# Second attention of a one-core decoder block: maxima subtracted through extra rows of the stacks, stacks copied by halves of the heads, score units further ahead, bias additions at another place

## The reference

```python
Q = query @ Wq.T + bq;  K = key @ Wk.T + bk;  V = value @ Wv.T + bv      # 16 heads of 8
energy = jnp.einsum('bhqd,bhkd->bhqk', Q, K) / jnp.sqrt(jnp.float32(HD))
attn = jax.nn.softmax(energy, axis=-1)
x = jnp.einsum('bhqk,bhkd->bhqd', attn, V)
return x @ Wo.T + bo
x = _layernorm(x + _L0_xattn_ref(x, ctx_1024, ctx_1024, ...), axis=-1)
```

## Time and profile before

| | us |
|---|---|
| median of 3 runs | 356.65 (356.54 to 357.73) |
| the profiled execution's own time | 357.19 |
| its span in the profile | 355.4 |
| PE busy / DVE / ACT / POOL | 326.9 / 250.7 / 190.7 / 215.4 |

### The profile page before, as it was taken

One profiled execution on the slowest core, in us unless ns is written; L12 is line 12 of the kernel. 1 busy time (PEld: TensorE's weight loads), 2 busy tenths in 40 slices (PEclk: granted clock), 3 DMA queues, 4 the chain that ended last, 5 costly groups with the idle time before them and its releaser, 6 DMA issues.

```text
span 355.4 us, 11656 instructions
## 1 busy us (share of the span) xinstructions
PE 326.9 (92%) x3728; PEld 259.1 (73%) x3728; DVE 250.7 (71%) x1220; ACT 190.7 (54%) x458; POOL 215.4 (61%) x402
## 2 busy tenths in 40 slices
PE   6989899998999999975799999998889999999993
PEld 3877788887888888864588887887646765666662
DVE  1688899988989999966367767769754279254454
ACT  3586566766676665575677767754643342222220
POOL 8375899998889977788733343311134445554552
PEclk9999999999999999999999999999999999999998
DMA  7669797775677688545454544641055300624310
GB/s 219 191 188 307 233 268 229 231 223 166 202 201 208 179 235 236 168 130 140 115 133 115 145 116 99 164 106 46 10 175 183 87 32 7 180 88 144 122 32 30
DMA packets 67808, 54.07 MB, mean 152 GB/s; under 512 B 29617, under 2 KB 57649, under 8 KB 67633
## 3 DMA queue, kind: packets, MB, share of 16 engines
q1 hardware_dynamic: 67328, 52.43, 51.9%
q10 hardware_dynamic: 432, 1.05, 0.9%
HBM read 33.40 MB, written 20.05 MB: 150 GB/s over the span
## 4 chain that ended last, share of the span: by engine, by line
PE 45%; POOL 16%; issue 11%; DVE 9%; DMA 9%; ACT 4%; SPq 4%; POOLq 0%; ACTq 0%; DVEq 0%
PE bank L844 6%; PE bank L1109 5%; DMA parts_dram<-parts 4%; PE bank L1113 4%; PE bank L784 4%; PE bank L1122 4%; DMA stk<-parts_dram 2%; PE bank L773 2%; POOL rstd L562 2%; PE bank L799 2%; POOL rest L498 2%; DMA sup_w<-in_sup_w_dram 2%; PE bank L828 2%; PE bank L821 2%; PE bank L787 2%
## 5 line engine op out<-in xcount | busy, mean ns | idle before, releaser
L707 POOL TENSOR_TENSOR stk<-stk 128x512 f32<-128x512 f32 x32 | 40.8, 1274 | 38.3 <-ACT stk L1434 35.4
L1227 ACT ACTIVATE prob_t<-bank 128x512 f32<-128x512 f32 x64 | 38.7, 605 | 41.6 <-PE bank L787 41.6
L1518 DVE CUSTOM_DVE_ANT_0 sums<-bank,decayed_e 128x128 f32<-128x128 f32 x256 | 59.1, 287 | 0.7
L1529 DVE TENSOR_REDUCE top<-bank 128x4 bf16<-128x512 f32 x64 | 43.9, 687 | 17.2 <-PE bank L799 16.9
L1236 ACT ACTIVATE prob_t<-bank 128x512 f32<-128x512 f32 x64 | 38.8, 606 | 26.7 <-PE bank L828 26.3
L1774 DVE TENSOR_TENSOR stk<-bank,stk 128x512 f32<-128x512 f32 x32 | 22.0, 691 | 39.2 <-POOL stk L707 38.0
L1434 ACT ACTIVATE stk<-bank 128x512 f32<-128x512 f32 x32 | 19.1, 597 | 53.6 <-PE bank L1109 53.6
L1506 DVE TENSOR_TENSOR decayed_e<-bank,decay 128x512 f32<-128x512 f32 x64 | 44.0, 687 | 2.5 <-issue 1.9
L498 POOL TENSOR_TENSOR rest<-pf,parts 128x256 f32<-128x256 f32 (+1 forms) x31 | 28.1, 908 | 28.9 <-ACT parts L1216 28.8
L844 PE MATMUL bank<-prob_t,vmix 128*32 128x128 f32 x1024 | 42.6, 278 | 2.2 <-ACT pvs L1253 2.2
L784 PE MATMUL bank<-ident,sums 128*128 128x128 f32 x256 | 39.3, 276 | 2.7 <-ACT prob_t L1227 1.2
(11 more groups left out here) (171 smaller groups left out, 756.6 us busy)
## 6 DMA issues: line engine op xcount, KB each, us to landing
stk<-parts_dram SPq DMA_DIRECT2D x32, 384.0 KB, 4.3
stk<-shares_dram SPq DMA_DIRECT2D x64, 128.0 KB, 2.9
parts_dram<-parts SPq DMA_DIRECT2D x32, 192.0 KB, 3.5
parts_dram<-parts SPq DMA_DIRECT2D x48, 128.0 KB, 3.1
stk<-parts_dram SPq DMA_DIRECT2D x32, 192.0 KB, 2.9
parts_dram<-parts SPq DMA_DIRECT2D x32, 96.0 KB, 2.3
parts_dram<-parts SPq DMA_DIRECT2D x48, 64.0 KB, 2.1
w<-in_w_dram SPq DMA_DIRECT2D x3, 512.0 KB, 5.6
```

The source lines that it names most:

```text
L707: pool.tensor_tensor(h1[kk % 2], sg[kk % 2], share[kk], ALU.mult).then_inc(weighted, 1)
L1227: act.activation(prob_t[g][:].rearrange("p h t -> p (h t)"), bank[3][:], ACT.Exp).then_inc(L1.exped, 1)
L1518: m = dve.tensor_tensor_reduce(out=sums[g % 2][:, j, :], in0=bank[g % 2][:, 128 * j:128 * j + 128], in1=decayed_e[:, g % 2, j, :], scale=1 ...
L1529: dve.tensor_reduce(top[:, b.par, GH * g:GH * g + GH], bank[S2_BANK[g % 2]][:].rearrange("p (h t) -> p h t", h=GH), AX.X, ALU.max).then_in ...
```

## The change

**Maxima.** Rows 96 to 111 of the key side of every stack hold a constant, -1.0058 in the columns of "their" head and 0 elsewhere (`pick_rows`, two DMAs at the start). A DMA on SP, `top_row`, copies `top_t` (16 x 128) into rows 96 to 111 of the query side, for each of the 16 heads: 16 x 16 pieces of 256 bytes. The transposed score product then subtracts the maximum (times 1.0058) by itself, and the L828 matmuls are gone. Softmax does not depend on the number subtracted. The untransposed scores need these rows at zero, so POOL clears them with a memset before a stack is used again (`clear_row`, batches 0 to 11), and the first score of a batch waits for it (`row_zero`).

**Copies.** `stack2` copies both sides of half the heads at a time. SP's order for each slot s is: row of batch s-1, first half-stack of s+2, four spills of s+3, second half-stack of s+2, last spill of s+3.

**Lead.** Scores and maxima run five units ahead in place of two; the maxima are turned at the end of a slot, into bank 4 in place of bank 6, and copied by ACT at the start of the next. On DVE, `unit2` stands before `unit1` in slots 0 to 3.

**Bias.** POOL's four bias additions come after slots 3, 5, 7 and 9. The loops of SP, POOL and DVE over the second attention are written out.

```diff
+            def pick_rows(p):
+
+                sp.wait_ge(zeroed[p], 1)
+                keys = stk[p][:].rearrange("p a h u t -> p (a h u t)").bitcast(F32)[TOP_ROW:TOP_ROW + H, H * S:2 * H * S]
+                sp.dma_start(keys.rearrange("p (k n) -> p k n", k=2),
+                             k["pick_rows"].unsqueeze(1).broadcast_to([H, 2, H * S // 2])).then_inc(in_rows_k, 16)
...
+            def stack2(b, half):
+
+                if half == 0:
+                    sp.wait_ge(L2.spilled[b.par], b.pair * L2.spill_step + L2.spill_step)
+                if b.n >= 4:
+                    sp.wait_ge(L2.shifted, NG * b.n - 4 * NG + NM + NM * half)
+                elif half == 0:
+                    sp.wait_ge(L1.scores, NG * NB - (NG if b.n == 0 else 0))
+                src = scr2[bass.ds(b.n, 1)].rearrange("b (a s) (f h) t -> (b s f) a h t", s=NP, h=H)
+                at = H // 2 * half
+                sp.dma_start(stk2[b.buf][0:2 * R:2, :, at:at + H // 2], src[:, :, at:at + H // 2]
+                             ).then_inc(L2.stacked[2 * b.buf + half], 16)
+
+            def top_row(b):
+
+                sp.wait_ge(L2.top_t_ev, b.n + 1)
+                sp.dma_start(stk2[b.buf][TOP_ROW:TOP_ROW + H, 0],
+                             top_t[0:H, b.par, :].unsqueeze(1).broadcast_to([H, H, S])).then_inc(L2.topped[b.par], 16)
...
+            for s in range(NB + 1):
+                if s >= 1:
+                    top_row(slot_batch(s - 1))
+                if s + 2 < NB:
+                    stack2(slot_batch(s + 2), 0)
+                if s + 3 < NB:
+                    spill_early(L2, slot_batch(s + 3))
+                if s + 2 < NB:
+                    stack2(slot_batch(s + 2), 1)
+                if s + 3 < NB:
+                    spill_late(L2, slot_batch(s + 3))
...
             def slot2(b):
+                c = b.back(3)
+                if c.live and c.n < NB - 4:
+                    clear_row(c)
+                    pool.wait_ge(L2.row_zero, c.n + 1)
...
+            for n in range(1, NB + 4):
+                if n < 4:
+                    last_slot1(NB + 1 + n, None)
                 slot2(slot_batch(n))
+                if n % 2 == 1 and 3 <= n < 11:
+                    residual_bias(2 * n - 6, 2 * n - 2)
...
+                if g == 0:
+                    pe.wait_ge(L2.topped[b.par], b.pair * 16 + 16)
                 for j in range(GH):
-                    pe.matmul(bank[2 + g % 2][:, 128 * j:128 * j + 128], stk2[b.buf][:, 1, head(g, j), :],
-                              stk2[b.buf][:, 0, head(g, j), :], start=(j == 0), stop=True,
-                              skip_group_check=True)
-                if g == 0:
-                    pe.wait_ge(L2.top_t_ev, b.n + 1)
-                for j in range(GH):
-                    h = GH * g + j
-                    m = pe.matmul(bank[2 + g % 2][:, 128 * j:128 * j + 128],
-                                  neg_ident[:, h:h + 1].broadcast_to([128, 128]), top_t[:, b.par, :],
-                                  start=False, stop=True, skip_group_check=True)
+                    m = pe.matmul(bank[2 + g % 2][:, 128 * j:128 * j + 128], stk2[b.buf][:, 1, head(g, j), :],
+                                  stk2[b.buf][:, 0, head(g, j), :], start=True, stop=True)
                 m.then_inc(L2.shifted, 1)
...
-                sb_, sg_ = unit_back(bb.back(1), g, -2)
+                sb_, sg_ = unit_back(bb.back(1), g, -5)
...
             for n in range(NB + 1, NB + 5):
                 for g in range(NG):
+                    unit2(slot_batch(n - NB - 1), g)
                     unit1(n // 2, n % 2, g)
-                    unit2(slot_batch(n - NB - 1), g)
```

More of the change, by code:

```diff
@@ L236, in __init__ @@
                 self.spilled = [sem(f"spilled{n}{p}") for p in range(2)]
-                self.stacked = [sem(f"stacked{n}{p}") for p in range(4)]
+                self.stacked = [sem(f"stacked{n}{p}") for p in range(4 * n)]
                 self.ent_scores = sem(f"ent_scores{n}")
@@ L425, in _ @@
             pair1(NB // 2 - 1)
[L427 to L430, removed]
-                    if b.back(-1).live:
-                        spill(L2, b.back(-1))
-            spill(L2, Batch2(0, 0))
-            load_ffn()
-            quad2(0)
-            with sp.Fori(1, 3) as q:
-                quad2(q)
-            quad2(3)
+            spill(L2, slot_batch(0))
+            load_ffn()
+            spill(L2, slot_batch(1))
+            stack2(slot_batch(0), 0)
+            stack2(slot_batch(0), 1)
+            spill(L2, slot_batch(2))
+            stack2(slot_batch(1), 0)
+            stack2(slot_batch(1), 1)
+            for s in range(NB + 1):
[9 more added lines that the diff above has]
+                    spill_late(L2, slot_batch(s + 3))
             def spill_shares(half):
@@ L652, in values2, with clear_row @@
                                  ).then_inc(L2.v_ready, 1)
+            def clear_row(b):
+                if b.n == 0:
+                    pool.wait_ge(root[1], NB)
+                elif b.n in (1, 3, 5, 7):
+                    pool.wait_ge(xb2, b.n // 2 + 1)
+                elif b.n < 11:
+                    pool.wait_ge(L2.low, b.n + 6)
+                else:
+                    pool.wait_ge(L2.v_ready, b.n + 2)
+                pool.wait_ge(L2.shifted, NG * b.n + NG)
+                pool.memset(stk2[b.buf][TOP_ROW:TOP_ROW + H, 0].rearrange("p h t -> p (h t)").bitcast(F32), 0.0
+                            ).then_inc(L2.row_zero, 1)
             def slot2(b):
+                c = b.back(3)
+                if c.live and c.n < NB - 4:
+                    clear_row(c)
+                    pool.wait_ge(L2.row_zero, c.n + 1)
                 if b.back(5).live:
@@ L919, in unit2 @@
                     out_product(L2, bb.back(4), xw_t[:, 3, :])
-                if g == 2 and bb.back(1).live:
-                    turn_top(bb.back(1))
+                if g == 3 and bb.live and (not isinstance(bb.n, int) or bb.n >= 1):
+                    turn_top(bb)
                 if g == 3 and bb.back(3).live:
@@ L1303, in unit2 @@
             def unit2(bb, g):
[L1304 removed]
+                if g == 0 and bb.back(1).live:
                     take_top(bb.back(1))
@@ L1460, in _ @@
             dve.memset(half_pi[:], math.pi / 2)
-            dve.memset(top_t[:].rearrange("p a t -> p (a t)").bitcast(F32), 0.0).then_inc(zeroed[2], 1)
             dve.wait_ge(L1.proj_done, 1)
@@ L1751, in scan @@
                 rstep(dve.tensor_tensor(r[dst][:, :, sh:NE], r[src][:, :, sh:NE], r[src][:, :, 0:NE - sh], ALU.add))
-            dve.wait_ge(xb2, 1)
-            slot2(slot_batch(4))
-            dve.wait_ge(xb2, 4)
-            with dve.Fori(1, 3) as q:
-                for i4 in range(1, 5):
-                    slot2(Batch2(q, 0).back(-i4))
-            for n in range(13, NB + 3):
+            for n in range(4, NB + 3):
+                if n % 4 == 0:
+                    dve.wait_ge(xb2, n // 4)
                 slot2(slot_batch(n))
```

110 lines of the change are left out of this document (55 added, 55 removed).

## The result

| | before | changed |
|---|---|---|
| median, us | 357.19 (356.54 to 358.75, 4 runs) | 367.91 (365.65 to 370.32, 4 runs) |
| ratio changed / before | | 1.030 (95%: 1.026 to 1.034) |
| the profiled execution's own time | 357.19 | 367.45 |
| its span | 355.4 | 365.7 |
| busy PE / DVE / ACT / POOL | 326.9 / 250.7 / 190.7 / 215.4 | 318.4 / 250.4 / 188.7 / 226.7 |

The change makes the kernel 3% slower. The forecast was 353.5 us, the range 347 to 358; the result lies outside, on the other side. PE has 8.5 us less to do, and that helps nothing.

What follows compares the result with a forecast made beforehand. Bounds: POOL's unbroken line in the hand-over, PE's loop through ACT in the slots, DVE late, DMA queue living on lead. Terms 0.5 + 3.0 - 2.7 - 1.5 - 2.1 - 0.4 = -3.2 from 357.19: 354.0, median 353.5 us; range 347 to 358.

Steps and rivals of the forecast that it cites:

- Start: Before slot 0: two DMAs write constant key rows, 128 KB each; 0 to 1.2 us, taken as +0.5.
- Hand-over against the change: Slots 0 to 3: maxima ahead of DVE's means delay POOL by 2.9, 1.3 and 0.5 us; whole hand-over +3.0.
- the bias additions: Hand-over: they leave POOL's line at three places before x1 is complete, 1.22 us each: -3.7.
- the memset: Hand-over: POOL clears 16 rows before batch 6's remainder; 0.9 us, 1.4 with the latencies for PE and ACT.
- Slots 4 to 11, and 12 to 13: Fewer bf16 matmuls on PE shorten the slots: -2.7 us in slots 4 to 11, -1.5 in 12 and 13.
- I take a mean period of 5.4: Slots 4 to 11: PE's period 5.28 us, raised to 5.4 for SP's cycle of 5.25 to 5.77; -2.7 us.
- PE's own loop: Slots 4 to 11: PE's shift, ACT's line to attn_ot, output product; period falls from 5.73 to 5.28 us.
- Rival C: Slots 4 to 11: the DMA queue becomes the bound, late rows stop PE; +3.5 for -2.7, 359.7 us; chance 0.13.
- The rule of the Trainium skill: DMA fixed cost about 2.0 us: wait after last spill 2.15 us, SP cycle 5.6, slots 4 to 11 -1.0.
- Slots 14 to 18: Three DVE maxima fewer in slots 14 to 16, -2.1 us; two groups fewer before the last exponent, -0.4.
- some 16 us: End: sign that the shares are ready some 16 us after slot 14 begins, before 18.
- rival A: Hand-over gains too, about -2.3 in place of +3.0, as DVE's new order is absorbed; 348.2 us; chance 0.25.

Runs made afterwards that it cites:

- row_act: Against the changed kernel: ACT issues the row DMA right after its copy of top_t, instead of SP in its order; 367.81 us, against 367.91.
- high_first: Against the changed kernel: SP issues the two high spills of batch s+3 ahead of the first half-stack of s+2; 358.59 us, against 367.91.
- dve_clear_high: Changed kernel with DVE's first-attention unit first in slots 0 to 3, batch 0's row cleared early, high spills before the half-stack; 351.37 us, against 367.91.

## Why the prediction was wrong

*Start.* +0.5 was forecast, -0.35 measured; the spread of slot 0's start is larger than both, so the term is neither shown nor refuted.

*Hand-over against the change.* The delays by DVE's order were worked out well: batch 13's mean "at 157.3" (POOL took it at 157.00), "POOL waits 2.9 us for it" (2.95), batch 14's at 164.4 (164.04), a third slot with 0.5 more (0.3). The stretch is nevertheless 2.8 us longer than forecast, for three reasons. First, the bias additions: -3.7 was set off against these delays as if both lay on one line. Alone it was worth 3.3, but in the changed kernel POOL waits 8.3 us for DVE, and the time that the additions leave free is spent in those waits: the last root starts 2.9 us late (177.41 against 174.48), not 1.0 as the terms without the clearing give. Second, the memset lasts 0.95 us as estimated (0.9), but its place was mispriced: I saw ACT and PE behind it, and not that it stands itself behind the last root, which the delays move. PE stood 3.6 us, of which 1.2 counted. Third, the clock: no term held it, and it was worth 1 to 2 us. These overlap, and no run splits the 2.8 us among them: with DVE's order put back alone, the hand-over is at 24.5 us, the value of the kernel before.

*Slots 4 to 11, and 12 to 13.* Here the forecast fell: -4.2 was forecast for both, +5.5 was measured. The step that failed is "I take a mean period of 5.4". PE's own loop was right: a stall of 0.6 before the output product (0.40 to 0.48 measured), and slots of 5.03 and 5.63 while the queue had lead. But the cycle of SP was taken as 5.25 to 5.77 us from the one best cycle of the earlier trace rows, although the same rows gave 6.36 over eight batches. It was 6.60: the wait from the last spill to the half-stack was 2.84 us in the mean where 1.78 to 2.30 was taken, and the issues from the half-stack to the last spill took 3.87 in the cycle shown above where the best cycle of the earlier trace rows had 3.47. The lead was gone after slot 6. That the row's issue is free in SP's wait was right (row_act), and no help.

Rival C named the mechanism, the place and the mark, and had 0.13. Its price, +3.5 in slots 4 to 11, was of the right kind (2.5 there, and 2.9 in slots 12 and 13, which it left out). The argument against it, "the slow issues come where four spills follow a whole stack", did not hold: most of the slowness was the wait for the landing of the last spill, which the new order left where it was; with two issues put into it (high_first) the cycle fell to 5.61. The rule of the Trainium skill that the prediction quoted ("DMA: Bandwidth & Descriptors", Anatomy of one DMA: a fixed part of about 2.0 us, mostly the receipt of the write) is stated there for DMAs issued by GpSimd, while these are issued by SP. The traces show the same kind of wait and a longer one: 2.49 and 2.60 us in the rows above and 2.84 in the mean, against the estimate of 2.15 by that rule. The cycle of 5.6 that the prediction worked out from it was a full microsecond short of 6.60.

*Slots 14 to 18.* -2.5 forecast, -0.6 measured. From slot 14 to the shares it took 16.65 us (247.66 to 264.31) in place of 18.11, so 1.5 less of the 2.1 forecast for DVE's maxima, and the prediction's own mark of "some 16 us" was nearly met. From the shares to the first up-projection it took 5.57 us in place of 4.73, where -0.4 was forecast. PE's clock was near its lower level there, and no term held that:

```profile
264.00:266.00 2.00, 1.69 (x21) 1.17 (x21) 1.06 (x4) 0.95 (x3) 0.04 (x1) 0.61 0.04 12
266.00:268.00 2.00, 2.00 (x15) 1.47 (x12) 0.22 (x1) 1.04 (x3) 0.00 (x0) 0.54 0.09 27
```

No row was late in these slots. With the queue put right (dve_clear_high) it takes 32.8 us from slot 12 to the first up-projection, against 35.9 before: 3.1 less, where -4.0 was forecast for slots 12 to 18. So the terms there were roughly right.

With its orders put right the change gives 351.4 us, 2 us under the forecast and 3 above rival A's 348.2. But about two thirds of that gain do not need it: 353.35 came from the kernel before by the bias and SP's order alone. The remaining 2.0 us, all that the maxima in the stacks, the halved copies and the longer lead can claim together, are hardly told from the spread: the four executions of one kernel took 352.74 to 354.85 us, those of the other 350.54 to 353.99.

## What to carry to other kernels

Before pricing a change of the compute engines, compare the period of the in-order DMA queue, averaged over many batches and not its best one, with that of the engine it feeds: a queue that lives on lead can take back what is gained upstream, as it did with the bias, and it shows as no wait until the lead is gone. In such a queue look first for the issue that waits for the landing of the one just before it, and put independent issues between them. And do not subtract work saved on an engine from a delay that makes the same engine wait: the saving ends in the wait.

## What was not expected of the hardware

The granted clock fell to the 1.2 GHz level for two thirds of 160 to 170 us after stalls of PE of at most 1.04 us each, while in the kernel before it stayed at 1.00 through a wait of 2.24; filling the waits with matmuls whose results nobody uses kept it at 1.00 from 160 to 190 us and shortened the hand-over by 2.0 us. A DMA issue on ACT's queue took 0.61 us, like the same one on SP's. The clearing of 16 partitions took 0.95 us for 1024 elements each, that of 128 partitions 3.51 us for 4096: the time went by the elements in a partition, and fewer partitions made it no cheaper.
